# Causal linear attention in quadrants of the TensorE array, with the quotients taken on GpSimd

## The chip, the cores and the metric

The kernel runs on one core of a Trainium2 chip. The metric is the device time of one execution in microseconds (us). The engines are TensorE (PE; its weight loads are PEld), VectorE (DVE), ScalarE (ACT), GpSimd (POOL) and SyncE (SP), each with its own in-order instruction stream; they wait for each other on semaphores.

## The reference

One decoder block over x of 128 sequences x 64 tokens x 128 features, 16 heads of 8 features: causal linear attention, a second attention over a context, and a layer of 8 experts with 2 taken per token. Only the first part is touched:

```
q, k = f(xn @ wq + bq), f(xn @ wk + bk)       f(x) = x + 1 where x > 0, else exp(x)
v    = xn @ wv + bv                           xn = layernorm(x)
S_t = sum over s <= t of k_s (x) v_s          z_t = sum over s <= t of k_s     (per head)
out_t = (q_t . S_t) / (q_t . z_t + 1e-6);     x = x + out @ wo + bo
```

## The kernel before

Tokens lie in 64 tiles of 128 (two sequences of 64 tokens each); four tiles (GT = 4) are a group, 16 groups in all. The work is a pipeline by slots, written out by hand for every engine (`slot(n, i)`): in slot n the engines do projections and features of group n+1 ("a1"), statistics and normalization of group n+2 ("a0"), running sums of group n ("b"), quotients and output projection of group n-1 ("c"), and the keys and gram matrices of the second attention for group n-2 ("d"). `slots` unrolls the first and last slots and loops over the middle. Each engine goes through its list strictly in order, so an instruction that waits holds everything behind it.

For tile t = 4g + k:

- TensorE `project` (L1344) makes q, k, v of the tile in one PSUM bank (384 columns). ScalarE `a_evac_proj` (L642) takes them out with two relus, a copy of v and an exp (L647 to L653).
- GpSimd `features` (L528) adds both halves to f(q), f(k) (`qk`, L534); `outer_product` (L536) multiplies the key with v and with a ninth column of ones (`v9`, L542), which gives 16 x 9 x 8 = 1152 products per token.
- TensorE `running_sums` (L1336) multiplies them by the lower triangle `tri_s` (block diagonal: two sequences), in three matmuls of 432, 360 and 360 columns into three PSUM banks (`HEADS`).
- VectorE `times_q` (L887) multiplies them by q, in three pieces (L896), and `sum_heads` (L900) sums over 8 (L905) into `nd`: 8 numerators and one denominator per head.
- A slot later, ScalarE `denominators` (L655) adds the epsilon, VectorE `inverses` (L927) takes the reciprocal, and VectorE `quotients` (L932) multiplies (L935); TensorE transposes the quotients (`transposes`, L1331), ScalarE copies them out (`oT`, L693), TensorE projects them and VectorE adds them to X (`add_attention`, L939).

What sets the order near the change: on TensorE a slot is: transposes of the next group's xh, running sums of tile 1, project 0, the second attention's keys (L1384), project 1, transposes of the quotients, running sums of tile 2, output projection, project 2, transposes of xh2, running sums of tile 3, project 3, running sums of tile 0 of the next group, gram. On ScalarE: xT, denominators, evacuation of project 0, oT (waits for the transposed quotients), evacuation 1, normalization of xh2 (L668, L671), k2T, x2T, evacuation 2, normalization of xh, evacuation 3, gd. On GpSimd: features 0, `variance` (L515, waits for the moments of L877), outer 0, features 1, `root` (L522), outer 1, features 2, variance, outer 2, features 3, root, outer 3.

`settle` (L296) raises a semaphore that nothing waits for. `need` waits only where the count is positive.

## Time and profile before

| | us |
|---|---|
| median of 3 runs (lowest, highest) | 632.59 (632.16, 632.62) |
| span of the profiled execution, first to last instruction | 631.7 |
| the attention stage in it | from about 18 to 270 |

The profiled execution has no time of its own beside its span; the three runs were timed without a profile, and the median is 0.9 us above the span, which is what lies around it. "Busy" is the union of an engine's instructions. A row of the timeline gives the start in us from the start of the span, the length in us, the engine, line, operation, out<-in, the count merged, and in brackets how long the engine had been idle before and what ended that. A matmul on fp32 data is recorded as two passes, each with its own weight load; rows of matmuls hold the time in which the last result drains.

### The profile page before, as it was taken

How to read it: one execution, taken by the hardware profiler on the slowest of the kernel's cores; microseconds unless marked ns; L12 is line 12 of the kernel's file. 1: busy time of each engine (PE TensorE's matmuls, PEld its weight loads, DVE VectorE, ACT ScalarE, POOL GpSimd, SP SyncE). 2: the span in 40 equal slices, each digit the busy share in tenths (PEclk: the TensorE clock that was granted, in tenths of full speed). 3: DMA queues.
4: the chain of work that ended last, by engine and by line, in shares of the span. 5: the costliest groups of instructions: out<-in, count | busy, mean ns of one | idle time of the engine just before them, and what ended most of it. 6: DMA issues, size and time to landing. Idle time of an engine off the chain costs nothing.

```text
span 631.7 us, 15833 instructions
## 1 busy us (share of the span) xinstructions
PE 575.6 (91%) x3838; PEld 442.8 (70%) x3839; DVE 517.9 (82%) x1602; ACT 420.2 (67%) x1188; POOL 427.0 (68%) x461
## 2 busy tenths in 40 slices
PE   3899999999999999968799877999999999999993
PEld 1455555555555555545689644799999999989993
DVE  5599999999999999983678888566877887877883
ACT  3557777877787777351788512345788888878882
POOL 2899989998999899310877600765467666757762
PEclk9999999999999999999999968899999999999998
DMA  5610111111161111283477551221012111111110
GB/s 147 184 51 0 35 33 35 34 33 33 33 100 33 34 33 34 66 119 90 119 208 202 113 113 29 53 51 46 27 49 54 48 47 47 51 38 51 51 44 23
DMA packets 49973, 40.92 MB, mean 65 GB/s; under 512 B 21971, under 2 KB 40278, under 8 KB 49926
## 3 DMA queue, kind: packets, MB, share of 16 engines
q1 hardware_dynamic: 44150, 29.61, 19.0%
q0 software_dynamic: 4960, 10.49, 6.4%
q8 instruction: 20, 0.33, 0.2%
q10 hardware_dynamic: 816, 0.26, 0.2%
q14 instruction: 27, 0.22, 0.1%
HBM read 27.47 MB, written 12.88 MB: 64 GB/s over the span
## 4 chain that ended last, share of the span: by engine, by line
PE 63%; ACT 12%; DVE 12%; issue 6%; DMA 4%; POOL 1%; DVEq 0%; ACTq 0%; SPq 0%; POOLq 0%
PE bank L1329 57%; PE bank L1333 4%; ACT xh L671 3%; ACT xs L773 2%; PE bank L1568 2%; DMA w_s<-gram_d 1%; DVE on L935 1%; ACT ex L647 1%; ACT nb_c L668 1%; DVE mean_early L1037 1%; DMA circ<-prob_d 1%; PE bank L1492 1%; ACT rl L648 1%; ACT xrT L759 1%; ACT ex L653 1%
## 5 line engine op out<-in xcount | busy, mean ns | idle before, releaser
L542 POOL TENSOR_TENSOR shared<-v,qk 128x1152 f32<-128x1152 f32 x64 | 142.8, 2231 | 2.8
L1329 PE MATMUL bank<-shared,tri_s 128*128 128x360 f32 (+1 forms) x384 | 137.2, 494 | 0.7 <-DVE R L896 0.7
L609 POOL DMA_INDIRECT shared<-xs_d,row_u x91 | 87.8, 964 | 62.2 <-DVE row_u L1227 31.6
L896 DVE TENSOR_TENSOR R<-bank,qk 128x360 f32<-128x360 f32 (+1 forms) x192 | 96.2, 540 | 8.6 <-PE bank L1329 6.7
L1329 PEld LDWEIGHTS bank<-shared,tri_s 128*128 128x128 f32 x384 | 69.8, 192 | 44.9 <-issue 20.4
L616 POOL DMA_INDIRECT out_x<-shared x64 | 63.6, 993 | 48.4 <-DVE shared L1299 21.8
L905 DVE TENSOR_REDUCE nd<-R 128x144 f32<-128x1152 f32 x64 | 86.1, 1346 | 1.6
L1329 PE MATMUL bank<-w_s,hid 128*128 (+1 forms) x620 | 82.3, 276 | 0.1
L1329 PEld LDWEIGHTS bank<-w_s,hid 128*128 128x128 f32 x620 | 75.5, 192 | 0.6 <-issue 0.3
L812 ACT ACTIVATE shared<-bank 128x256 f32<-128x256 f32 x155 | 59.4, 384 | 21.9 <-PE bank L1329 16.2
L1320 DVE TENSOR_TENSOR hid<-bank,shared 128x256 f32<-128x256 f32 x155 | 61.4, 422 | 10.0 <-ACT shared L812 9.8
L1329 PE MATMUL bank<-shared,ct 128*128 128x128 f32 x512 | 67.8, 275 | 0.0
L1329 PE MATMUL bank<-shared,u 128*128 128x128 f32 x512 | 67.6, 275 | 0.0
L1329 PE MATMUL bank<-wqkv,xT 128*128 128x384 f32 x128 | 56.7, 526 | 6.9 <-ACT v L650 4.6
L1329 PEld LDWEIGHTS bank<-shared,ct 128*128 128x128 f32 x512 | 62.2, 192 | 0.3 <-issue 0.2
L1329 PEld LDWEIGHTS bank<-shared,u 128*128 128x128 f32 x512 | 62.3, 192 | 0.0
L802 ACT ACTIVATE shared<-bank,scale_s 128x128 f32<-128x128 f32 (+1 forms) x78 | 30.1, 386 | 41.1 <-PE bank L1568 41.1
L534 POOL TENSOR_TENSOR qk<-ex,rl 128x256 f32<-128x256 f32 x64 | 48.0, 751 | 9.7 <-ACT ex L653 9.6
L647 ACT ACTIVATE ex<-bank 128x256 f32<-128x256 f32 x64 | 24.1, 376 | 36.2 <-PE bank L1329 36.2
L1329 PEld LDWEIGHTS bank<-wqkv,xT 128*128 128x128 f32 x128 | 22.5, 198 | 29.7 <-ACT v L650 21.6
L806 ACT ACTIVATE ct<-w_s 128x512 f32 x64 | 39.7, 620 | 0.1
L1329 PE MATMUL bank<-ones 128*128 128x512 bf16 x128 | 36.0, 423 | 0.0
(247 smaller groups left out, 1138.4 us busy)
## 6 DMA issues: line engine op xcount, KB each, us to landing
xs_d<-xs SPq DMA_DIRECT2D x16, 270.0 KB, 4.7
X<-in_x SPq DMA_DIRECT2D x16, 256.0 KB, 2.8
ct<-in_ctx_t SPq DMA_DIRECT2D x16, 256.0 KB, 2.8
ct<-in_ctx_r SPq DMA_DIRECT2D x16, 256.0 KB, 3.6
gram_d<-gd SPq DMA_DIRECT2D x14, 256.0 KB, 2.4
w_s<-in_w_experts SPq DMA_DIRECT2D x8, 384.0 KB, 4.0
circ<-prob_d SPq DMA_DIRECT2D x30, 64.0 KB, 2.7
shared<-xs_d,row_u POOLq DMA_INDIRECT x91, 2.6
```

The lines of the kernel that those rows point to most:

```text
L534: nc.gpsimd.tensor_tensor(qk[p][:, k, :], ex[k % 2][:], rl[k % 2][:], ALU.add).then_inc(a_f, 1)
L542: nc.gpsimd.tensor_tensor(outer[k], v9[k % 2][:].unsqueeze(3).broadcast_to([P, H, D1, D]), kk.unsqueeze(2).broadcast_to([P, H, D1, D]), AL ...
L609: nc.gpsimd.indirect_dma_start(xg[q], None, xs_d[:, :], bass.IndirectOffsetOnAxis(ap=rows, axis=0)).then_inc(xg_in[q], 16)
L616: nc.gpsimd.indirect_dma_start(out[:, :], bass.IndirectOffsetOnAxis(ap=xg[(NXI + j) % NX][:, DEST:DEST + 1].bitcast(U32), axis=0), yg[q], ...
L647: nc.scalar.activation(ex[k % 2][:], bank[1][:, 0:2 * E], ACT.Relu, scale=-1.0).then_inc(a_pev, 1)
L802: nc.scalar.activation(xgT[p][:, cols], bank[0][:, cols], ACT.Copy, scale=scale_s[:, 0:1]).then_inc(x_xT, 1)
L806: nc.scalar.activation(w_tile[n % 2][0], w_s[:, dyn(held[0] * W_E, 2 * HID)], ACT.Copy).then_inc(x_wa, 1)
L812: nc.scalar.activation(silu[p][h], bank[1 + 2 * p + h][:, HID:2 * HID], ACT.Silu).then_inc(x_silu, 2 // len(items_of(i, up[0])))
L896: nc.vector.tensor_tensor(R[:, lo:hi], bank[2 + c][:, 0:n_h * D1 * D].rearrange("p (h e d) -> p h e d", h=n_h, e=D1), qq.unsqueeze(2).broa ...
L905: nc.vector.tensor_reduce(nd[p][:, k], R[:], AX.X, ALU.add).then_inc(b_red, 1)
L1320: nc.vector.tensor_tensor(hid[p][h][:], bank[1 + 2 * p + h][:, 0:HID], silu[p][h], ALU.mult).then_inc(x_h, 2 // len(items_of(i, j)))
L1329: return nc.tensor.matmul(o, l, r, start=start, stop=stop, skip_group_check=True)
```

## The change

The ninth column goes: `v8` holds v alone, an outer product has 1024 products per token, and the two running-sum banks `run` take the place of three. `running_sums` becomes four matmuls of 512 columns, each on 64 rows and 64 columns of the array: for sequence b of the tile and half c of the heads, from partitions of b to partitions of c. So partitions hold (half of the heads, token) and columns hold (sequence, ...). q is projected in the same layout by four matmuls of 64 columns, k and v as before by one of 256. `times_q` is one instruction per tile, `sum_heads` sums 1024 to 128. The denominators come apart from this: `key_sums` runs once per group on TensorE, at the slot's head ahead of the running sums of tile 1, waits for the features of all four tiles and sums the keys (four matmuls of 256 columns into bank 4); VectorE `key_dots` multiplies them by q and `sum_dots` sums them; ScalarE adds the epsilon in the group's own slot, behind evacuation 2, and VectorE takes the inverses in front of the last `sum_heads`. `quotients` is the first instruction of GpSimd's slot. `turn_quotients` turns them back with 16 matmuls of 64 columns by the identity in place of four transposes.

```diff
@@ -127,16 +126,16 @@
         xh = sb("xh", [P, GT, E])
         xT = sb("xT", [P, GW])
         ex, rl = [sb(f"ex{i}", [P, 2 * E]) for i in range(2)], [sb(f"rl{i}", [P, 2 * E]) for i in range(2)]
-        v9 = [sb(f"v9_{i}", [P, H, D1]) for i in range(2)]
+        v8 = [sb(f"v8_{i}", [P, E]) for i in range(2)]
         qk = [sb(f"qk{i}", [P, GT, 2 * E]) for i in range(2)]
 
-        shared = sb("shared", [P, GT * H * D1 * D])
+        shared = sb("shared", [P, 9 * GT * E])
         bias_f, bias_r, bias_a, bias_b = (shared[0:3, i * NBIAS:(i + 1) * NBIAS] for i in range(4))
         b_wide = shared[:, 4 * NBIAS:4 * NBIAS + 3 * E]
-        outer = [shared[:, i * H * D1 * D:(i + 1) * H * D1 * D].rearrange("p (h e d) -> p h e d", h=H, e=D1)
-                 for i in range(GT)]
-        R = sb("R", [P, H, D1, D])
-        nd = [sb(f"nd{i}", [P, GT, H, D1]) for i in range(2)]
+        outer = [shared[:, i * D * E:(i + 1) * D * E] for i in range(GT)]
+        R = sb("R", [P, (D + 1) * E])
+        num = [sb(f"num{i}", [P, GT, E]) for i in range(2)]
+        zq = sb("zq", [P, GT * E])
         den, rden = sb("den", [P, GT * H]), sb("rden", [P, GT * H])
         on = sb("on", [P, GT, E])
         oT = sb("oT", [P, GW])
...
@@ -537,11 +541,20 @@
                 t = GT * g + k
                 pool.wait_ge(a_f, t + 1)
                 pool.wait_ge(a_pev, 3 * t + 3)
-                need(pool, b_run, 3 * (t - GT) + 3)
+                need(pool, b_run, t - GT + 1)
                 kk = qk[p][:, k, E:2 * E].rearrange("p (h d) -> p h d", h=H)
+                vv = v8[k % 2][:].rearrange("p (h e) -> p h e", h=H)
                 nc.gpsimd.tensor_tensor(
-                    outer[k], v9[k % 2][:].unsqueeze(3).broadcast_to([P, H, D1, D]),
-                    kk.unsqueeze(2).broadcast_to([P, H, D1, D]), ALU.mult).then_inc(a_outer, 1)
+                    outer[k].rearrange("p (h e d) -> p h e d", h=H, e=D), vv.unsqueeze(3).broadcast_to([P, H, D, D]),
+                    kk.unsqueeze(2).broadcast_to([P, H, D, D]), ALU.mult).then_inc(a_outer, 1)
+
+            def quotients(g, p, r):
+                pool.wait_ge(c_rden, g + 1)
+                need(pool, c_tr, g)
+                pool.wait_ge(b_red, GT * g + GT)
+                nc.gpsimd.tensor_tensor(
+                    on[:].rearrange("p t (h d) -> p (t h) d", h=H), num[p][:].rearrange("p t (h d) -> p (t h) d", h=H),
+                    rden[:].unsqueeze(2).broadcast_to([P, GT * H, D]), ALU.mult).then_inc(c_on, 1)
 
             def slot(n, i):
                 a0, a1, c = stage(n, i, 2), stage(n, i, 1), stage(n, i, -1)
...
@@ -549,6 +562,8 @@
                 of_c = c and (c[0], c[1], mv_c, c_mv, ve_c, c_ve, rs_c, c_rs, d_xh)
                 if i is None and n == -1:
                     pool.wait_ge(bias_ch, 8)
+                if c:
+                    quotients(*c)
                 if a1:
                     features(*a1, 0)
                 if a0:
...
@@ -647,15 +662,13 @@
                 nc.scalar.activation(ex[k % 2][:], bank[1][:, 0:2 * E], ACT.Relu, scale=-1.0).then_inc(a_pev, 1)
                 nc.scalar.activation(rl[k % 2][:], bank[1][:, 0:2 * E], ACT.Relu).then_inc(a_pev, 1)
                 need(act, a_outer, t - 1)
-                nc.scalar.activation(v9[k % 2][:, :, 0:D], bank[1][:, 2 * E:3 * E].rearrange("p (h d) -> p h d", h=H),
-                                     ACT.Copy).then_inc(a_pev, 1)
+                nc.scalar.activation(v8[k % 2][:], bank[1][:, 2 * E:3 * E], ACT.Copy).then_inc(a_pev, 1)
                 act.wait_ge(a_pev, 3 * t + 1)
                 nc.scalar.activation(ex[k % 2][:], ex[k % 2][:], ACT.Exp, scale=-1.0).then_inc(a_ex, 1)
 
             def denominators(g, p, r):
-                act.wait_ge(b_red, GT * g + GT)
-                need(act, c_rden, g)
-                nc.scalar.activation(den[:], nd[p][:, :, :, D].rearrange("p t h -> p (t h)"), ACT.Copy, bias=ATT_EPS).then_inc(c_den, 1)
+                act.wait_ge(b_dots, 2 * g + 2)
+                nc.scalar.activation(den[:], den[:], ACT.Copy, bias=ATT_EPS).then_inc(c_den, 1)
 
             def negative_mean(g, p, mv, mv_sem, mr, mr_sem):
                 act.wait_ge(mv_sem, GT * g + GT)
...
@@ -681,8 +694,6 @@
                     nc.scalar.activation(wvo_s[:], bank[1][:, 0:E], ACT.Copy).then_inc(fold_w, 1)
                 if a1:
                     a_evac_xT(*a1)
-                if c:
-                    denominators(*c)
                 if d:
                     negative_mean(d[0], d[1], mv_c, c_mv, mr_c, c_mr)
                 if a1:
@@ -705,6 +716,8 @@
                     nc.scalar.activation(x2T[:], bank[5][:], ACT.Copy).then_inc(d_xT, 1)
                 if a1:
                     a_evac_proj(*a1, 2)
+                if b:
+                    denominators(*b)
                 if a0:
                     g, p, r = a0
                     need(act, a_tr, g)
...
@@ -884,25 +897,35 @@
                 for k in range(GT):
                     nc.vector.bn_aggr(mv_e[:, GT * g + k, :], st_e[:, k, :]).then_inc(e_mv, 1)
 
-            def times_q(g, p, r, k, pieces):
+            def times_q(g, p, r, k):
                 t = GT * g + k
-                if pieces[0] == 0:
-                    need(dve, b_red, t)
-                for c in pieces:
-                    lo, hi = HEADS[c]
-                    n_h = hi - lo
-                    dve.wait_ge(b_run, 3 * t + c + 1)
-                    qq = qk[p][:, k, lo * D:hi * D].rearrange("p (h d) -> p h d", h=n_h)
-                    nc.vector.tensor_tensor(
-                        R[:, lo:hi], bank[2 + c][:, 0:n_h * D1 * D].rearrange("p (h e d) -> p h e d", h=n_h, e=D1),
-                        qq.unsqueeze(2).broadcast_to([P, n_h, D1, D]), ALU.mult).then_inc(b_mul, 1)
+                need(dve, b_red, t)
+                dve.wait_ge(b_run, t + 1)
+                qq = qk[p][:, k, 0:E].rearrange("p (h d) -> p h d", h=H)
+                nc.vector.tensor_tensor(
+                    R[:, 0:D * E].rearrange("p (h e d) -> p h e d", h=H, e=D),
+                    run[:].rearrange("p (h e d) -> p h e d", h=H, e=D),
+                    qq.unsqueeze(2).broadcast_to([P, H, D, D]), ALU.mult).then_inc(b_mul, 1)
 
             def sum_heads(g, p, r, k):
                 t = GT * g + k
-                dve.wait_ge(b_mul, 3 * t + 3)
+                dve.wait_ge(b_mul, t + 1)
                 if k == 0:
                     need(dve, c_on, g - 1)
-                nc.vector.tensor_reduce(nd[p][:, k], R[:], AX.X, ALU.add).then_inc(b_red, 1)
+                nc.vector.tensor_reduce(num[p][:, k, :], R[:, 0:D * E].rearrange("p (x d) -> p x d", d=D), AX.X, ALU.add
+                                        ).then_inc(b_red, 1)
+
+            def key_dots(g, p, r):
+
+                dve.wait_ge(b_keys, g + 1)
+                nc.vector.tensor_tensor(
+                    zq[:].rearrange("p (k b x) -> p b k x", k=GT, b=2), bank[4][:].rearrange("p (b k x) -> p b k x", b=2, k=GT),
+                    qk[p][:, :, 0:E].rearrange("p k (b x) -> p b k x", b=2), ALU.mult).then_inc(b_dots, 1)
+
+            def sum_dots(g, p, r):
+                dve.wait_ge(b_dots, 2 * g + 1)
+                need(dve, c_rden, g)
+                nc.vector.tensor_reduce(den[:], zq[:].rearrange("p (x d) -> p x d", d=D), AX.X, ALU.add).then_inc(b_dots, 1)
 
             def split_fold():
 
...
@@ -946,23 +962,18 @@
             def slot(n, i):
                 a0, a1, b, c = (stage(n, i, s) for s in (2, 1, 0, -1))
                 if b:
-                    times_q(*b, 0, (0, 1, 2))
+                    times_q(*b, 0)
                 if b:
                     sum_heads(*b, 0)
-                if c:
-                    inverses(*c)
-                if b:
-                    times_q(*b, 1, (0,))
-                if c:
-                    quotients(*c)
-                if b:
-                    times_q(*b, 1, (1, 2))
+                    key_dots(*b)
+                    times_q(*b, 1)
                 if a0:
                     g, p, r = a0
                     dve.wait_ge(x_in[p], 16 * r + 16)
                     stats(g, p, st_a, a_st, mv_a, a_mv, a_nb, GT)
                 if b:
                     sum_heads(*b, 1)
+                    sum_dots(*b)
                 if a0:
                     moments(a0[0], a0[1], st_a, a_st, mv_a, a_mv, a_nb, GT)
                 if i is None and n == FIRST:
...
@@ -984,11 +995,11 @@
                     dve.wait_ge(c_x1, c[0] + 1)
                     stats(c[0], c[1], st_c, c_st, mv_c, c_mv, c_nb, GT)
                 if b:
-                    times_q(*b, 3, (0,))
+                    times_q(*b, 3)
                 if c:
                     moments(c[0], c[1], st_c, c_st, mv_c, c_mv, c_nb, GT)
                 if b:
-                    times_q(*b, 3, (1, 2))
+                    inverses(*b)
                     sum_heads(*b, 3)
 
...
@@ -1333,20 +1344,49 @@
                     last = nc.tensor.transpose(o[:, k * P:(k + 1) * P], src[:, k, :], id_s[:])
                 return last
 
+            def turn_quotients():
+
+                settle(pe)
+                for k in range(GT):
+                    for b in range(2):
+                        for c in range(2):
+                            own = slice(c * HALF, c * HALF + HALF)
+                            last = mm(bank[5][own, k * P + b * HALF:k * P + b * HALF + HALF],
+                                      on[own, k, b * HALF:b * HALF + HALF], id_s[own, own])
+                return last
+
             def running_sums(g, p, r, k):
                 t = GT * g + k
                 pe.wait_ge(a_outer, t + 1)
-                for c, (lo, hi) in enumerate(HEADS):
-                    need(pe, b_mul, 3 * (t - 1) + c + 1)
-                    mm(bank[2 + c][:, 0:(hi - lo) * D1 * D], tri_s[:], outer[k][:, lo:hi].rearrange("p h e d -> p (h e d)")
-                       ).then_inc(b_run, 1)
+                need(pe, b_mul, t)
+                settle(pe)
+                for b in range(2):
+                    for c in range(2):
+                        own = slice(b * L, b * L + L)
+                        last = mm(run[c * L:c * L + L, b * 512:b * 512 + 512], tri_s[own, own], outer[k][own, c * 512:c * 512 + 512])
+                last.then_inc(b_run, 1)
+
+            def key_sums(g, p, r):
+
+                pe.wait_ge(a_f, GT * g + GT)
+                need(pe, b_dots, 2 * g - 1)
+                for b in range(2):
+                    for c in range(2):
+                        last = mm(bank[4][c * L:c * L + L, b * GT * HALF:(b + 1) * GT * HALF], tri_s[:, b * L:b * L + L],
+                                  qk[p][:, :, E + c * HALF:E + c * HALF + HALF])
+                last.then_inc(b_keys, 1)
 
             def project(g, p, r, k):
                 t = GT * g + k
                 if k == 0:
                     pe.wait_ge(a_xT, g + 1)
                 need(pe, a_pev, 3 * t)
-                mm(bank[1][:, 0:3 * E], xT[:, k * P:(k + 1) * P], wqkv[:]).then_inc(a_proj, 1)
+                mm(bank[1][:, E:3 * E], xT[:, k * P:(k + 1) * P], wqkv[:, E:3 * E])
+                for b in range(2):
+                    for c in range(2):
+                        last = mm(bank[1][c * L:c * L + L, b * HALF:b * HALF + HALF], xT[:, k * P + b * L:k * P + b * L + L],
+                                  wqkv[:, c * HALF:c * HALF + HALF])
+                last.then_inc(a_proj, 1)
 
             def keep_warm(of, times):
 
...
@@ -1370,6 +1410,7 @@
                     need(pe, a_xT, a1[0])
                     transposes(bank[0], xh).then_inc(a_tr, 1)
                 if b:
+                    key_sums(*b)
                     running_sums(*b, 1)
                 if a1:
                     if i is None and a1[0] == 0:
...
@@ -1385,11 +1426,11 @@
                 if a1:
                     project(*a1, 1)
                 if i is None and n == NG:
-                    pe.wait_ge(b_mul, 3 * NT)
+                    pe.wait_ge(b_mul, NT)
                     keep_warm(2, 10)
                 if c:
                     pe.wait_ge(c_on, c[0] + 1)
-                    transposes(bank[5], on).then_inc(c_tr, 1)
+                    turn_quotients().then_inc(c_tr, 1)
                 if i is None and n == NG:
                     keep_warm(2, 2)
                 if b:
```

## Rows read from the trace of the kernel before

**Rows 1.** The page of the profile: busy time of the engines over the span.
```profile
PE 575.6 (91%) x3838; PEld 442.8 (70%) x3839; DVE 517.9 (82%) x1602; ACT 420.2 (67%) x1188; POOL 427.0 (68%) x461
...
PE 63%; ACT 12%; DVE 12%; issue 6%; DMA 4%; POOL 1%; DVEq 0%; ACTq 0%; SPq 0%; POOLq 0%
```

**Rows 2.** Engines by stretch: busy of PE, PEld, DVE, ACT, POOL; clock; DMA share; GB/s.
```profile
60.00:100.00 40.00, 38.44 (x188) 22.63 (x188) 38.97 (x89) 32.23 (x106) 35.88 (x31) 1.00 0.09 27
```

**Rows 3.** Timeline, feature tile 3 of groups 1, 2, 14, 15 on POOL: start, us.
```profile
39.51 0.73 POOL L534 TENSOR_TENSOR qk<-ex,rl 128x256 f32<-128x256 f32 x1
...
53.81 0.72 POOL L534 TENSOR_TENSOR qk<-ex,rl 128x256 f32<-128x256 f32 x1
...
239.93 0.73 POOL L534 TENSOR_TENSOR qk<-ex,rl 128x256 f32<-128x256 f32 x1
...
253.30 0.73 POOL L534 TENSOR_TENSOR qk<-ex,rl 128x256 f32<-128x256 f32 x1
```

**Rows 4.** Timeline of one slot, TensorE from one gram to the quotients, and ScalarE.
```profile
66.22 0.69 PE L1329 MATMUL bank<-x2T,k2T 128*64 128x64 f32 x16
...
66.83 0.66 PE L1333 MATMUL bank<-id_s,xh 128*128 128x128 f32 x4
...
67.33 2.10 PE L1329 MATMUL bank<-shared,tri_s 128*128 128x432 f32 x6
...
68.02 0.31 ACT L658 ACTIVATE den<-nd 128x64 f32<-128x64 f32 x1
...
69.26 0.81 PE L1329 MATMUL bank<-wqkv,xT 128*128 128x384 f32 x2
...
69.91 1.02 PE L1329 MATMUL bank<-ct,wkk 128*128 128x512 f32 x2
70.11 0.38 ACT L647 ACTIVATE ex<-bank 128x256 f32<-128x256 f32 x1 [1.68 <-PE bank L1329]
...
70.99 0.91 PE L1329 MATMUL bank<-wqkv,xT 128*128 128x384 f32 x2
...
71.74 0.60 PE L1333 MATMUL bank<-id_s,on 128*128 128x128 f32 x4
...
72.38 0.60 ACT L693 ACTIVATE oT<-bank 128x512 f32<-128x512 f32 x1 [1.14 <-PE bank L1333]
```

**Rows 5.** The same timeline, later: the rest of the slot on ScalarE, VectorE, GpSimd.
```profile
71.22 0.86 DVE L869 BATCH_NORM_STATS2 st_a<-X 128x6 f32<-128x128 f32 x4
...
72.00 1.33 DVE L905 TENSOR_REDUCE nd<-R 128x144 f32<-128x1152 f32 x1
...
73.25 0.37 DVE L877 BATCH_NORM_AGGREGATE mv_a<-st_a 128x2 f32<-128x6 f32 x4
...
73.81 0.19 POOL L520 TENSOR_SCALAR ve_a<-mv_a 128x4 f32<-128x4 f32 x1 [0.66 <-ACT v L650]
...
81.33 1.49 DVE L896 TENSOR_TENSOR R<-bank,qk 128x432 f32<-128x432 f32 x3
...
81.78 0.41 ACT L653 ACTIVATE ex<-ex 128x256 f32<-128x256 f32 x1
...
82.02 0.66 PE L1333 MATMUL bank<-id_s,xh 128*128 128x128 f32 x4
...
83.26 0.73 POOL L534 TENSOR_TENSOR qk<-ex,rl 128x256 f32<-128x256 f32 x1
```

**Rows 6.** Groups of instructions, 60 to 246 us: count, busy us, mean ns, idle before.
```profile
L935 DVE TENSOR_TENSOR on<-nd,rden 128x512 f32<-128x512 f32 x12 | 13.8, 1150 | 0.0
...
L526 POOL TENSOR_TENSOR rs_a<-ve_a,power 128x4 f32<-128x4 f32 x12 | 12.2, 1021 | 0.0
```

**Rows 7.** Timeline: the quotients on VectorE beside an outer product on GpSimd.
```profile
84.94 2.17 POOL L542 TENSOR_TENSOR shared<-v,qk 128x1152 f32<-128x1152 f32 x1
...
85.12 2.53 DVE L935 TENSOR_TENSOR on<-nd,rden 128x512 f32<-128x512 f32 x1
```

**Rows 8.** Timeline of the last slots: the last quotients and what follows them.
```profile
269.68 0.60 ACT L693 ACTIVATE oT<-bank 128x512 f32<-128x512 f32 x1 [1.96 <-PE bank L1333]
```

More of the change, by code:

```diff
@@ L53 @@
 PITCH = L * (2 * L + 1)
-HEADS = [(0, 6), (6, 11), (11, 16)]
+HALF = E // 2
 def need(eng, sem, count):
@@ L221, in build @@
         is_row = [halves(shared[:, SORT + i * NSORT * NT:SORT + (i + 1) * NSORT * NT], PAIRS, 2, NT, 2) for i in range(2)]
-        is_tile = [halves(R[:].rearrange("p h e d -> p (h e d)")[:, i * PAIRS * NT:(i + 1) * PAIRS * NT], PAIRS, NT, 2)
+        is_tile = [halves(R[:][:, i * PAIRS * NT:(i + 1) * PAIRS * NT], PAIRS, NT, 2)
                    for i in range(2)]
-        row_t = R[:].rearrange("p h e d -> p (h e d)")[:, NSORT * NT:NSORT * NT + P]
+        row_t = R[:][:, NSORT * NT:NSORT * NT + P]
         xg = [shared[:, i * ROW:(i + 1) * ROW] for i in range(NX)]
@@ L236, in build, with psum @@
         y0 = sb("y0", [P, E])
-        bank = [ctx.enter_context(nc.psum_tensor(f"bank{i}", [P, 512], F32)) for i in range(8)]
+        def psum(name, banks=1):
+            return ctx.enter_context(nc.psum_tensor(name, [P, banks * 512], F32))
+        bank = [psum("bank0"), psum("bank1")]
+        run = psum("run", 2)
+        bank += [run[:, i * 512:(i + 1) * 512] for i in range(2)] + [psum(f"bank{i}") for i in range(4, 8)]
         settled = sem("settled")
@@ L256, in build @@
         b_run, b_mul, b_red = sem("b_run"), sem("b_mul"), sem("b_red")
+        b_keys, b_dots = sem("b_keys"), sem("b_dots")
         c_den, c_rden, c_on, c_tr, c_oT, c_y, c_x1, c_st, c_mv, c_ve, c_rs = (
@@ L505, in _ @@
             pool.memset(power[:], -0.5).then_inc(setup, 1)
-            for k in range(2):
-                pool.memset(v9[k][:], 1.0).then_inc(setup, 1)
             pool.memset(ones_f[:], 1.0).then_inc(setup, 1)
@@ L512, in _ @@
             pool.memset(used[0][:], 0.0).then_inc(s_used, 1)
-            pool.wait_ge(setup, 5)
+            pool.wait_ge(setup, 3)
             def variance(g, p, stats, seen, ve, ve_sem, rs, rs_sem, normed):
@@ L531, in features @@
                 pool.wait_ge(a_ex, t + 1)
-                need(pool, b_mul, 3 * (t - 2 * GT) + 3)
+                need(pool, b_mul, t - 2 * GT + 1)
+                need(pool, b_dots, 2 * (g - 1) - 1)
                 need(pool, a_outer, t - 2 * GT + 1)
@@ L674, in slot @@
             def slot(n, i):
-                a0, a1, c, d = (stage(n, i, s) for s in (2, 1, -1, -2))
+                a0, a1, b, c, d = (stage(n, i, s) for s in (2, 1, 0, -1, -2))
                 if i is None and n == 1:
@@ L930, in inverses @@
                 nc.vector.reciprocal(rden[:], den[:]).then_inc(c_rden, 1)
-            def quotients(g, p, r):
-                dve.wait_ge(c_rden, g + 1)
-                need(dve, c_tr, g)
-                nc.vector.tensor_tensor(
-                    on[:].rearrange("p t (h d) -> p (t h) d", h=H), nd[p][:, :, :, 0:D].rearrange("p t h d -> p (t h) d"),
-                    rden[:].unsqueeze(2).broadcast_to([P, GT * H, D]), ALU.mult).then_inc(c_on, 1)
             def add_attention(g, p, r):
@@ L977, in slot @@
                 if b:
-                    times_q(*b, 2, (0, 1, 2))
+                    times_q(*b, 2)
                 if c:
@@ L1006, in _ @@
             nc.vector.tensor_scalar(rev[:], iota_s[:, 0:NE], -1.0, float(NE), ALU.mult, ALU.add).then_inc(setup, 1)
-            dve.wait_ge(setup, 12)
+            dve.wait_ge(setup, 10)
             dve.wait_ge(s_used, 1)
@@ L1439, in _ @@
             pe.wait_ge(const_in, 64)
-            pe.wait_ge(setup, 5)
+            pe.wait_ge(setup, 3)
             mm(bank[1][:, 0:3 * E], ones_f[:], wqkv[:]).then_inc(w_mean, 1)
@@ L1450, in v_product @@
                 last.then_inc(e_v, 1)
-            pe.wait_ge(b_mul, 3 * NT)
+            pe.wait_ge(b_mul, NT)
             pe.wait_ge(fold_w, 1)
@@ L1515, in cross_slot @@
                         keep_warm(0, 3)
-            pe.wait_ge(setup, 11)
+            pe.wait_ge(setup, 9)
             cross_slots(cross_slot)
```

1 line of the change is left out of this document (removed).

## The prediction

> **What bounds the kernel now.** I read the page first. TensorE has the largest busy share and the largest share of the chain [rows 1], but that mixes stages; the change touches the attention stage alone, so the table of engines by stretch counts. There TensorE is busy 38.4 us of 40, VectorE 39.0, GpSimd 35.9, ScalarE 32.2, at the full granted clock [rows 2]. Two engines are full, so taking work from both looks like a sure gain. The length of a slot comes from a fixed mark: the fourth features instruction of a group on GpSimd (F3 below) starts at 53.81 for group 2 and at 239.93 for group 14 [rows 3]: 186.1 us for 12 slots, **15.51 us a slot**. The timeline of one slot then shows who waits for whom. ScalarE goes from oT (72.38) to the last exp of project 3 (81.78 + 0.41 = 82.19) in 9.81 us, nearly all of it its own work [rows 4, 5]. VectorE reaches its next slot at 81.33; F3 ends only at 83.26 + 0.73 = 83.99, though its input was there at 82.19, because GpSimd was in an outer product; and TensorE starts its slot with transposes at 82.02 [rows 5]. So a group's last features come 2.0 us *after* TensorE has entered the slot of that group. Today this costs nothing: the running sums of tile 1 need only tile 1.
>
> **By busy time** the change gains. An outer product takes 2.17 us for 1152 elements [rows 7] and a features instruction 0.73 for 256 [rows 3]: 1.61 ns an element beside 0.32 fixed. So 1024 elements cost 1.97 us, and the quotients (512) 1.14; bounds are 0.96 (share of an outer product) and 1.46 (twice features), and I take the line through both. GpSimd has per slot 4 x 1.97 + 4 x 0.73 + 2 roots of 1.02 [rows 6] + 2 x 0.19 [rows 5] + 1.14 = 14.4 us. VectorE: busy 15.1 (0.974 x 15.51); three pieces of times_q take 1.49 together [rows 5], so one of 1024 costs 1.49 less 0.13 less two starts of 0.1 = 1.17: minus 1.3 per slot; four sums of 128 x 8 instead of 144 x 8 save 0.13 each: 0.5; the quotients go, 1.15 on average [rows 6], since some of them last 2.53 beside an outer product [rows 7]; two new instructions of 512 add about 0.68 each. Sum 13.5. TensorE: a full-array pass of 512 columns takes (1.02 - 0.17)/2 = 0.43, where 0.17 is the drain by which neighbours overlap (67.33 + 2.10 against 69.26) [rows 4]. The gram's 16 passes of 64 columns would take 16 x 0.053 = 0.86 in a row, but take 0.69 - 0.17 = 0.52 [rows 4]: its two column halves run at once. For the row halves no row exists. Bounds for the four quadrants' running sum: 0.87 (all four at once, two passes of 0.43) and 1.73 (only column pairs); I take 0.87, as the gram's pairs overlap almost fully. After the gram, neighbours overlap by 0.08, not 0.17 (66.22 + 0.69 against 66.83) [rows 4]: I take 0.1 for each change of the array's shape. There are some 14 more per slot. TensorE comes to about 13 us. So no engine is fuller than 14.4 of today's 15.5.
>
> **By the round trip** it loses, and that decides. `key_sums` stands at the head of TensorE's slot and waits for F3; behind it in the same queue are running sums 1, project 0, project 1 and the turning of the quotients, for which ScalarE's oT waits; and behind oT are 9.81 us of ScalarE work that end in the exp that the *next* F3 needs. Everything is in order, so this is a closed circle of one slot. From the end of F3, in us: 0.10 to wake TensorE and load; keys 0.86 (four matmuls of 256 columns, two at once, two passes of 0.213); 0.10 shape; running sum 0.87; 0.10; k and v 0.43; 0.10; q 0.23; 0.21 drain and wake; ScalarE's relus and v copy with the wake 0.88 (70.11 to 70.99) [rows 4]; project 1 0.43 + 0.10 + 0.23; 0.10; turning 0.93 (16 matmuls, two passes of 0.053 to 0.058, two quadrants at once, where four transposes took 0.44); 0.21. Sum **5.88** to the start of oT. Before, without keys and shapes, transposes to oT took 66.83 to 72.38. Then 9.81, plus 0.31 for the epsilon instruction, now inside that stretch [rows 4], 0.05 to wake, 0.73 for F3: 5.88 + 9.81 + 0.31 + 0.05 + 0.73 = **16.78 us a slot**.
>
> The other engines fit in. Quotients: GpSimd after F3 has a root 1.02, outer 1.97, quotients 1.14: ready at 4.2, before TensorE gets there (4.8). So moving them neither gains nor loses in a full slot; cover 0.6 us. GpSimd with VectorE makes a second circle: F3, keys, running sum, times_q 1 at 2.14; then 1.17, statistics 0.78, sum 1.12, denominators' sum 0.68, moments 0.56 to the variance [rows 5]; from variance to F3's end 10.18 (73.81 to 83.99) less three shortenings of 0.2: 9.57. Sum 16.0, also above 15.51. It sets a slot where ScalarE has less: slot 1 (before: 53.81 - 39.51 = 14.30) and slot 14 (253.30 - 239.93 = 13.37) [rows 3], which I put at 16.0 and 15.9.
>
> Sum: 12 x (16.78 - 15.51) = +15.2; slot 1 +1.7; slot 14 +2.5; two shorter outer products ahead of the first F3, -0.4. The end, from F3 of group 15 (254.03) to the last oT (269.68) [rows 3, 8]: shorter by three tiles of 0.45 and the denominators' 0.8, longer by keys 0.96, turning 0.5, quotients 0.46 and a wake: no difference. Setup loses two small fills of `v9`, covered by loads. After 270 us nothing changes. +19.0 on the profiled 631.7 and so on the median of 632.6 (0.9 above it): **651.6 us**.
>
> **Rivals.** (a) Quadrants that share one bank are not written at once: turning takes 1.8, 0.9 more on the circle, 13 slots and the end: +13, 664 us. For it: both turning quadrants write bank 5 from different rows of the array; against: the gram's halves share bank 6 and overlap [rows 4], though from the same rows. The page TensorEngine Tiling (Array Packing) of the Trainium skill, Restrictions and Gotchas, says that different row tiles cannot access one PSUM bank simultaneously; no row of before shows it. (b) Row halves don't overlap anywhere: also +0.87 for running sum 1, and TensorE itself fills: 18.6 us a slot, about 676. (c) **Faster**, one mechanism: the wait of the keys doesn't bind, because F3 is there when TensorE has done its transposes. Then GpSimd's 14.4 sets the slot: 12 x (14.4 - 15.5) and 2 at the ends, about 617. It decides once F3 ends before about 0.5 after TensorE's slot begins; today it ends 2.0 after, 1.1 of which is GpSimd's lateness, and the 0.73 and the exp before it can't go. (d) The circle is 1.3 shorter than I add up (no cost of shapes, shorter wakes, gains of the ends): no change.
>
> **Numbers.** The forecast case 0.62, (a) 0.14, (b) 0.09, (c) 0.10, (d) 0.05. Small terms: without shape costs the circle is 16.2 (-8 us, and -2 at slots 1 and 14): 641; (a) with slower quotients (1.46) 668. Range 641 to 668; it leaves out (b), (c), (d) in the main. 0.2% is what a measurement of this kernel can tell from no change. Slower 0.86, same 0.03, faster 0.11.
>
> **What would show it.** In the profile after: F3 to F3 at 16.8; "PE <- POOL qk" as a large new wait in front of the keys' weight load, some 1 us a slot; VectorE busy near 80% in the stretch, idle in front of key_dots; ScalarE's wait for oT longer; running sum of a tile about 1.04 long in place of 2.10; quotients on GpSimd 1.14 and ahead of TensorE. I am wrong if keys are found without a wait, if F3 follows GpSimd's own work rather than the exp, or if slots are below 15.5.

## The result, and the profile after

The median after is 663.35 us (662.79 to 666.04, four runs) against 632.54 before: ratio 1.0489 [1.0466, 1.0512]. The forecast was slower, 651.6 us, range 641 to 668: the sign and the range hold, but the loss is 30.8 us, not 19.0. The profiled span grew from 631.7 to 661.4, by 29.7.

The page after, for [rows 1], with the groups of the changed work (busy us, mean ns | idle before, releaser):

```profile
PE 563.1 (85%) x5054; PEld 418.3 (63%) x5055; DVE 498.8 (75%) x1490; ACT 417.3 (63%) x1188; POOL 425.6 (64%) x475
...
PE 39%; DVE 8%; ACT 3%; DMA 3%; issue 2%; POOL 1%; DVEq 0%; ACTq 0%; SPq 0%; POOLq 0%
...
L547 POOL TENSOR_TENSOR shared<-v,qk 128x1024 f32<-128x1024 f32 x64 | 125.0, 1953 | 2.8
L905 DVE TENSOR_TENSOR R<-run,qk 128x1024 f32<-128x1024 f32 x64 | 78.4, 1224 | 45.4 <-PE run L1340 43.8
...
L915 DVE TENSOR_REDUCE num<-R 128x128 f32<-128x1024 f32 x64 | 76.8, 1200 | 1.1
```

Engines by stretch after (length; busy of PE, PEld, DVE, ACT, POOL; clock, DMA share, GB/s), for [rows 2]:

```profile
60.00:100.00 40.00, 34.22 (x365) 18.19 (x365) 32.62 (x68) 26.55 (x91) 31.98 (x31) 1.00 0.09 28
...
180.00:220.00 40.00, 33.59 (x318) 16.45 (x316) 31.04 (x63) 24.86 (x84) 30.85 (x28) 0.96 0.33 63
```

No engine is full any more: VectorE fell from 39.0 to 32.6 of 40 us, and the kernel is slower. Who waits, 60 to 260 us (total us, times, longest):

```profile
ACT ex L662 <- PE bank L1340: 41.8, 12, 4.9
DVE R L905 <- PE run L1340: 28.1, 35, 1.5
ACT oT L704 <- PE bank L1340: 23.9, 12, 2.0
...
PE bank L1340 <- POOL qk L538: 14.9, 11, 1.4
```

The last row is the wait of the keys: 11 slots of some 1.3 us. The first and third are where ScalarE pays for it: 3.5 us a slot in front of project 0's relu and 2.0 in front of oT, where the same view of the kernel before has 20.6 and 16.4 us in all, 1.7 and 1.4 a slot. One turn of the circle, from the timeline, from F3 to the next F3:

```profile
91.05 0.72 POOL L538 TENSOR_TENSOR qk<-ex,rl 128x256 f32<-128x256 f32 x1 [0.37 <-ACT ex L667]
...
91.91 1.08 PE L1340 MATMUL bank<-qk,tri_s 128*64 128x256 f32 x8 [1.22 <-POOL qk L538]
...
92.92 1.09 PE L1340 MATMUL run<-shared,tri_s 64*64 64x512 f32 x8
...
93.94 1.08 PE L1340 MATMUL bank<-wqkv,xT 128*128 128x256 f32 x10
94.64 1.07 POOL L555 TENSOR_TENSOR on<-num,rden 128x512 f32<-128x512 f32 x1
...
95.15 0.38 ACT L662 ACTIVATE ex<-bank 128x256 f32<-128x256 f32 x1 [3.11 <-PE bank L1340]
...
96.03 1.08 PE L1340 MATMUL bank<-wqkv,xT 128*128 128x256 f32 x10
...
97.04 1.08 PE L1340 MATMUL bank<-id_s,on 64*64 64x64 f32 x29
...
98.31 0.60 ACT L704 ACTIVATE oT<-bank 128x512 f32<-128x512 f32 x1 [2.04 <-PE bank L1340]
...
107.86 0.41 ACT L667 ACTIVATE ex<-ex 128x256 f32<-128x256 f32 x1
...
108.51 0.73 POOL L538 TENSOR_TENSOR qk<-ex,rl 128x256 f32<-128x256 f32 x1 [0.61 <-DVE R L905]
```

Read downwards, this is the forecast's chain link by link: F3 ends at 91.77, the keys start at 91.91, and everything up to oT follows without a gap of its own; ScalarE needs 9.96 us from oT to the end of the exp, and F3 comes 0.24 later. The quotients are ready at 95.71, ahead of TensorE's 97.04. F3 starts at 39.35 for group 1, 56.94 for group 2, 266.81 for group 14 and 283.46 for group 15: slot 1 is 17.59 us, slot 14 is 16.65, and the 12 between are **17.49** on average (209.87 in all) (forecast 16.0, 15.9 and 16.78; before [rows 3] 14.30, 13.37 and 15.51).

### The profile page after: what moved, and what is told of

It reads as the page before. It is cut to its first block, busy times and chain, and to the rows that moved or that the text cites. A ratio compares the mean times of both kernels' runs of the same rounds, so it can differ in the third digit from the quotient of the medians.

```text
span 661.4 us, 18060 instructions
## 1 busy us (share of the span) xinstructions
PE 563.1 (85%) x5054; PEld 418.3 (63%) x5055; DVE 498.8 (75%) x1490; ACT 417.3 (63%) x1188; POOL 425.6 (64%) x475
## 4 chain that ended last, share of the span: by engine, by line
PE 39%; DVE 8%; ACT 3%; DMA 3%; issue 2%; POOL 1%; DVEq 0%; ACTq 0%; SPq 0%; POOLq 0%
PE bank L1340 25%; PE run L1340 11%; ACT xs L786 2%; PE bank L1609 2%; DMA w_s<-gram_d 1%; DVE mean_early L1048 1%; PE run L1533 1%; DVE st_e L895 1%; ACT xrT L772 1%; DVE X L1169 1%; DMA circ<-prob_d 0%; DMA shared<-xs_d,row_u 0%; DMA gram_d<-gd 0%; POOL rs_e L605 0%; DVE base L1209 0%
## 5 line engine op out<-in xcount | busy, mean ns | idle before, releaser
L547 POOL TENSOR_TENSOR shared<-v,qk 128x1024 f32<-128x1024 f32 x64 | 125.0, 1953 | 2.8
L905 DVE TENSOR_TENSOR R<-run,qk 128x1024 f32<-128x1024 f32 x64 | 78.4, 1224 | 45.4 <-PE run L1340 43.8
L1340 PEld LDWEIGHTS bank<-wqkv,xT 128*64 128x64 f32 (+1 forms) x640 | 41.0, 153 | 72.2 <-issue 37.5
L1340 PE MATMUL bank<-wqkv,xT 128*64 128x64 f32 (+1 forms) x640 | 71.3, 280 | 10.8 <-ACT v L665 10.0
L915 DVE TENSOR_REDUCE num<-R 128x128 f32<-128x1024 f32 x64 | 76.8, 1200 | 1.1
L1340 PE MATMUL run<-shared,tri_s 64*64 64x512 f32 x512 | 72.9, 632 | 1.6 <-issue 1.5
L1331 DVE TENSOR_TENSOR hid<-run,shared 128x256 f32<-128x256 f32 x78 | 33.0, 423 | 7.8 <-ACT shared L825 7.4
L825 ACT ACTIVATE shared<-run 128x256 f32<-128x256 f32 x78 | 29.8, 382 | 10.9 <-PE run L1340 7.7
L825 ACT ACTIVATE shared<-bank 128x256 f32<-128x256 f32 x77 | 29.5, 383 | 10.6 <-PE bank L1340 8.4
L1340 PE MATMUL run<-shared,ct 128*128 128x128 f32 x256 | 33.9, 275 | 0.1
L1340 PE MATMUL run<-shared,u 128*128 128x128 f32 x256 | 33.8, 275 | 0.0
```

The costliest lines, as they stand in the source:

```text
L547: nc.gpsimd.tensor_tensor(outer[k].rearrange("p (h e d) -> p h e d", h=H, e=D), vv.unsqueeze(3).broadcast_to([P, H, D, D]), kk.unsqueeze(2 ...
L825: nc.scalar.activation(silu[p][h], bank[1 + 2 * p + h][:, HID:2 * HID], ACT.Silu).then_inc(x_silu, 2 // len(items_of(i, up[0])))
L905: nc.vector.tensor_tensor(R[:, 0:D * E].rearrange("p (h e d) -> p h e d", h=H, e=D), run[:].rearrange("p (h e d) -> p h e d", h=H, e=D), q ...
L915: nc.vector.tensor_reduce(num[p][:, k, :], R[:, 0:D * E].rearrange("p (x d) -> p x d", d=D), AX.X, ALU.add).then_inc(b_red, 1)
L1331: nc.vector.tensor_tensor(hid[p][h][:], bank[1 + 2 * p + h][:, 0:HID], silu[p][h], ALU.mult).then_inc(x_h, 2 // len(items_of(i, j)))
L1340: return nc.tensor.matmul(o, l, r, start=start, stop=stop, skip_group_check=True)
```

## The experiments

Theory C (the closed circle of the forecast) says that a slot is F3, keys, TensorE's order up to oT, and ScalarE's order up to the next F3. The rivals were that GpSimd's new piece costs the time, and that the narrow matmuls do. All kernels start from the changed one unless said otherwise; ratios are to the kernel before on the same chip. In the cuts of code, words in round brackets and behind `#` stand for lines or places that are not printed.

**The keys later.** On TensorE behind the running sums of tile 2; their multiply and sum on VectorE behind those of tile 2.

```diff
-                    key_sums(*b)
                     running_sums(*b, 1)
...
                     running_sums(*b, 2)
+                    key_sums(*b)
```

> Edit to the changed kernel: the key sums go behind the running sums of tile 2 on TensorE, key_dots and sum_dots behind times_q 2 and sum_heads 2 on VectorE. Theory (circle through the keys' wait): features no longer hold TensorE's slot head. The circle of 17.4 us opens; the next one goes oT, 9.9 us of ScalarE, features 3, root, outer product, quotients on GpSimd (0.2 + 0.7 + 1.0 + 1.95 + 1.1), turning 1.3: about 16.3 us a slot, 13 slots: 648 us (644 to 653). Rival (the many small matmuls and their changes of shape fill TensorE): the place of the keys doesn't matter, 660 or more. Rival (VectorE and GpSimd set the slot): no change either.

Measured 645.87 us (643.87 to 646.47), ratio 1.0202 [1.0180, 1.0224]. oT comes every 16.13 to 16.28 us in place of 17.4. The place of one wait costs 17.5 us of the 30.8. The matmuls of the keys are all still there, so this is the wait and not their work; what remains is +13. Some 1.6 of the 17.5 comes from the clock: this trace has one stretch at a lower clock, the changed kernel has two (both told further below).

**The quotients back on VectorE,** behind the first `times_q`; the keys stay at the head.

```diff
-                if c:
-                    quotients(*c)        # GpSimd, slot's head
...
                     times_q(*b, 0)
+                if c:
+                    quotients(*c)        # VectorE
```

> Edit to the changed kernel: the quotients alone go back to VectorE, behind times_q 0; the rest stays. Theory (circle through the keys): quotients are ready before TensorE gets to them on either engine, so 663 us within 4. Rival (quotients at GpSimd's slot head cost the time): back to about 640.

Measured 672.98 us (669.55 to 674.10), ratio 1.0619 [1.0587, 1.0651]: 9.6 *above* the changed kernel, where no difference was expected. The timeline shows F3 and the quotients side by side:

```profile
93.23 1.28 POOL L538 TENSOR_TENSOR qk<-ex,rl 128x256 f32<-128x256 f32 x1 [0.37 <-ACT ex L657]
93.25 0.68 DVE L949 TENSOR_TENSOR on<-num,rden 128x512 f32<-128x512 f32 x1
...
94.64 1.08 PE L1340 MATMUL bank<-qk,tri_s 128*64 128x256 f32 x8 [1.78 <-POOL qk L538]
```

Here F3 takes 1.28 us in place of 0.73, on the circle. This is the worst slot: where the quotients start some 0.25 before F3, as in nine of the slots, F3 takes 1.02 to 1.03:

```profile
111.00 0.68 DVE L949 TENSOR_TENSOR on<-num,rden 128x512 f32<-128x512 f32 x1
...
111.25 1.02 POOL L538 TENSOR_TENSOR qk<-ex,rl 128x256 f32<-128x256 f32 x1 [0.60 <-DVE R L895]
```

Ordinary slots are 17.68 to 17.85 us, 0.3 longer like F3: some 3.7 us in 12 slots. Five of the slots are 18.98 to 19.35; in each of them the granted clock falls. The trace has four such stretches more than that of the changed kernel, at some 1.6 us each: 6.4 of the 10.9 us by which the two profiled spans differ. In the changed kernel the move of the quotients is thus worth 9.6 us, which the forecast put at nothing, but only some 3.7 us of it are the collision of the two engines.

**Both together.**

> Edit to the changed kernel: keys late and quotients on VectorE, both. Theory: both circles through GpSimd are open; the rest is oT, ScalarE up to the normalized group (8.9), transposes, running sum 1, project 0, ScalarE, project 1, turning: about 15.7 us a slot, 640 us (634 to 646), below keys late alone by some 8. Rival (VectorE and GpSimd set the slot, where the quotients on VectorE collide with outer products): not below keys late alone.

Measured 639.48 us (638.79 to 640.61), ratio 1.0111 [1.0094, 1.0128]. With late keys the quotients on VectorE are 6.4 us *better* than on GpSimd (645.87), with early keys 9.6 worse: what the move is worth hangs on which circle binds. Here the slots alternate between 15.99 and 16.19, not the 15.7 expected: with F3 off the path, the one pair of `run` banks binds, since a running sum waits until VectorE has multiplied the one before:

```profile
116.12 1.23 DVE L895 TENSOR_TENSOR R<-run,qk 128x1024 f32<-128x1024 f32 x1
...
117.49 1.09 PE L1340 MATMUL run<-shared,tri_s 64*64 64x512 f32 x8 [0.89 <-DVE R L895]
```

**The quotients alone, on the kernel before,** at the head of GpSimd's slot.

> Edit to the kernel before: only the quotients go to GpSimd's slot head. Theory: the circle oT, 9.8 us of ScalarE, features 3 to quotients on GpSimd (5.2), turning (0.75) is about 15.7 to 15.9 a slot against 15.5: 635 to 640 us. Rival (VectorE was the bound and is freed of 1.15 us a slot, collisions included): 620 to 628.

Measured 637.78 us (636.95 to 639.76), ratio 1.0090 [1.0067, 1.0112]. The busiest engine is relieved and the kernel loses 5 us. GpSimd is busy 37.9 of 40 us in the stretch of [rows 2], in place of 35.9, and slots go to 15.75.

**q in the old layout:** one projection of 384 columns. `times_q` then multiplies by q of other tokens and heads, so the attention's values differ; every instruction keeps its shape.

```diff
-                mm(bank[1][:, E:3 * E], xT[:, k * P:(k + 1) * P], wqkv[:, E:3 * E])
-                (four matmuls of 64 columns)
+                mm(bank[1][:, 0:3 * E], xT[:, k * P:(k + 1) * P], wqkv[:]).then_inc(a_proj, 1)
```

> Edit to the changed kernel: q, k and v of a tile again by one matmul of 384 columns (q then lies in the old layout, so the attention is not the reference's; no instruction but the projection changes). Two projections lie on the circle; from their start to ScalarE's first relu they now take 1.21 us against 0.85 before, and from project 1 to the turning 1.01 against 0.75. Theory (the circle's terms add): 0.62 us a slot less, 16.8 us a slot, 13 slots: 663.4 - 8 = 655 (652 to 658). Rival (TensorE's total work sets the slot): all four projections count, 1.45 us a slot less, 644.

Measured 659.40 us (657.72 to 660.69), ratio 1.0410 [1.0376, 1.0445], above both expectations and 1.4 outside the range of the first.

```profile
94.46 0.91 PE L1340 MATMUL bank<-wqkv,xT 128*128 128x384 f32 x2
...
96.37 0.91 PE L1340 MATMUL bank<-wqkv,xT 128*128 128x384 f32 x2
97.21 1.08 PE L1340 MATMUL bank<-id_s,on 64*64 64x64 f32 x29
```

From project 1 to the turning it is 0.84 us where it was 1.01, from project 0 to the relu 1.03 (in the same timeline the relu starts at 95.49) where it was 1.21: q's own matmuls cost 0.17 to 0.18 a tile against one wide one, and the slot falls by 0.37 (17.42 to 17.05), where 0.62 was expected: that took both stretches back to their lengths before, 0.85 and 0.75. In the kernel before the same wide project 1 takes 0.75 to the transposes behind it, without a change of shape [rows 4: 70.99 to 71.74]. So 0.09 of the 0.84 is the change of shape, as the forecast's 0.10 has it.

**Running sums on the full array:** two matmuls of 512 columns in place of four, which leaves the sums in the old layout of partitions.

> Edit to the changed kernel: the running sums by two matmuls of 512 columns on the whole array in place of four in the quadrants (the sums then lie in the old layout, so the attention is not the reference's). One running sum lies on the circle: 4 x 0.43 = 1.71 us of streaming in place of about 0.92, a change of shape less. Theory: 0.7 us a slot more, 672 us (668 to 677). Rival (the quadrants don't run at once, or their gain lies elsewhere): no change, 661 to 665. Rival (TensorE full): four running sums count, 2.8 us a slot, 700.

Measured 674.62 us (674.08 to 675.84), ratio 1.0666 [1.0635, 1.0697]; slots 18.14, +0.72. So the four quadrants run at once, and the one running sum on the circle is 0.7 shorter by them. Of the change's parts this is the one that pays where it binds.

**Late keys, and the quotients on GpSimd behind F3 of the slot before** in place of the head.

> Edit to the kernel with late keys: GpSimd takes the quotients of the finished group behind features 3, ahead of the root and the last outer product, no longer at the next slot's head. Theory (second circle, through root and outer product ahead of the quotients): it opens as it did with quotients on VectorE, 639 us or a little less, since VectorE loses 0.8 us a slot of work (636 to 641). Rival (GpSimd's total work sets the slot): as with late keys alone, 646.

Measured 640.19 us (639.37 to 642.74), ratio 1.0129 [1.0093, 1.0165]: 5.7 less than with the quotients at the head. At the head they stood between an outer product and the next slot's first features with no gap on either side (in the run with late keys 105.76 to 106.79), and so made GpSimd late by their own length.

**A new order.** On top of that: the second attention's keys and project 0 ahead of the running sum of tile 1, ScalarE's copy of the gram behind the first evacuation of the next slot, features wait for the exp last; two more slots are written out ahead of the loop.

```diff
-                    running_sums(*b, 1)
-                    project(*a1, 0)
                     (keys of the second attention)
+                    project(*a1, 0)
+                    running_sums(*b, 1)
                     project(*a1, 1)
```

> Edit to the kernel of the run before this one: on TensorE the second attention's keys and project 0 go ahead of running sum 1, which had waited for times_q 0; ScalarE's gram copy goes behind evacuation 0 of the next slot, into its wait; features wait for the exp last; the loop over slots starts two slots later. Theory (what is left is ScalarE's own chain: oT to the last exp 9.9, xT 0.6, project 0 1.2, evacuation 0.9, project 1 1.0, turning 1.3 = 14.9, and VectorE's 14.2 with its waits): 15.2 us a slot, 626 to 633. Rival (the chain stays on VectorE and running sums, one buffer for both): 636 to 640.

Measured 627.05 us (624.78 to 629.50), ratio 0.9897 [0.9865, 0.9929]. Slots are 14.72 us where written out and 15.0 to 15.2 in the loop. With this order the changed kernel beats the one before by 1.0%.

**The same order on the kernel before,** as a control.

> Edit to the kernel before (full-array sums, quotients on VectorE): the same new order as in the reordered kernel, as a control: the second attention's keys and project 0 ahead of running sum 1, the gram copy behind evacuation 0, the loop two slots later. Theory: before is held by TensorE's 14.9 us and VectorE's 15.1 us of work in a slot of 15.5, so an order that shortens ScalarE's round trip gives little: 628 to 634. Rival (the order alone makes the gain of the reordered kernel): 627 or less.

Measured 635.43 us (631.89 to 637.46, ten runs), ratio 1.0034 [1.0015, 1.0053], just above the range expected. Its ordinary slots are 15.0 to 15.2 and two are 16.9. So the order alone gains nothing in the whole; it needs the room that the change made. In its trace groups 2 to 14 take 184.2 us in place of 186.1, a gain of 1.9 us, and slot 1 takes 16.4 in place of 14.3 at a granted clock of 0.58 (40 to 44 us), a loss of the same size. The control lacks the late wait of the features, which by itself shows no gain (last run).

**The new order without a loop:** all slots written out.

```diff
-            for n in range(FIRST, 6):
-                slot(n, None)
-            with eng.Fori(3, (NG - 2) // 2) as i:
-                slot(0, i)
-                slot(1, i)
-            for n in range(NG - 2, LAST + 1):
+            for n in range(FIRST, LAST + 1):
```

> Edit to the reordered kernel: no loop over slots, all are written out. In its trace the written-out slots take 14.72 us, those in the loop 15.08 (waits against registers stand on the circle). Theory: 8 slots of 0.36 us: 3 us less, 624 (621 to 626). Rival (the longer program costs its own fetches): 627 or more.

Measured 622.96 us (621.44 to 626.17), ratio 0.9837 [0.9801, 0.9874], the fastest of all. oT comes every 14.72 to 14.73 us, slot after slot. Three engines are at 37 to 38 of 40 us, against 32 to 34 in the changed kernel:

```profile
100.00:140.00 40.00, 37.79 (x410) 20.28 (x409) 36.78 (x77) 32.04 (x108) 37.65 (x36) 1.00 0.14 41
```

**The features' wait for the exp last,** alone on the changed kernel.

```diff
-                pool.wait_ge(a_ex, t + 1)
                 (the other waits)
+                pool.wait_ge(a_ex, t + 1)
                 nc.gpsimd.tensor_tensor(qk[p][:, k, :], ex[k % 2][:], rl[k % 2][:], ALU.add)
```

> Edit to the changed kernel: in features the wait for the exp stands last, behind the three waits that are long fulfilled. In the changed kernel's trace features 3 starts 0.24 to 0.37 us behind the exp's end. Theory (that start lies on the circle): 0.2 us a slot less, 660.5 (659 to 662). Rival: no change, 663.4.

Measured 663.98 us (661.18 to 665.02), ratio 1.0471 [1.0444, 1.0498]: no gain to be seen. The slots are 17.22 and 17.39 in turn in place of 17.38 and 17.46, about 0.1 shorter, but two of them are 18.8 and 19.0, where the changed kernel had one of 19.05. A gain of 1 us is less than the 1.6 that one such slot costs. Inconclusive.

## Why the prediction was right, and why 12 us short

**The chain was right, its links were too short.** The circle by links, in us: the forecast, a written-out slot (F3 at 74.00 and 91.05) and a loop slot (the one shown above).

| link | forecast | written out | loop |
|---|---|---|---|
| F3 end to keys | 0.10 | 0.05 | 0.14 |
| keys to running sum 1 | 0.96 | 1.02 | 1.01 |
| running sum 1 to project 0 | 0.97 | 1.01 | 1.02 |
| project 0 to relu | 0.97 | 1.13 | 1.21 |
| relu to project 1 | 0.88 | 0.88 | 0.88 |
| project 1 to turning | 0.86 | 1.01 | 1.01 |
| turning to oT | 1.14 | 1.20 | 1.27 |
| oT to end of exp | 10.12 | 9.95 | 9.96 |
| exp to F3 | 0.05 | 0.07 | 0.24 |
| F3 | 0.73 | 0.73 | 0.72 |
| slot | 16.78 | 17.05 | 17.46 |

The rows of the written-out slot that the shown ones don't cover:

```profile
74.00 0.73 POOL L538 TENSOR_TENSOR qk<-ex,rl 128x256 f32<-128x256 f32 x1 [0.37 <-ACT ex L667]
...
74.78 1.08 PE L1340 MATMUL bank<-qk,tri_s 128*64 128x256 f32 x8 [1.15 <-POOL qk L538]
...
77.94 0.38 ACT L662 ACTIVATE ex<-bank 128x256 f32<-128x256 f32 x1 [2.97 <-PE bank L1340]
...
79.83 1.08 PE L1340 MATMUL bank<-id_s,on 64*64 64x64 f32 x29
...
81.03 0.60 ACT L704 ACTIVATE oT<-bank 128x512 f32<-128x512 f32 x1 [1.96 <-PE bank L1340]
```

Three terms failed, one by its size and two that were put at nothing:

1. *The length of a projection.* The forecast summed 0.76 for either projection, 0.12 above the 0.64 that the wide project 0 takes [rows 4: 69.26 to 69.91]. q's own matmuls cost 0.17 (the run with q in the old layout), and project 1 takes 0.10 more than project 0 already in the kernel before [rows 4: 70.99 to 71.74]; why is not shown. That is the 0.15 of the row "project 1 to turning". For project 0 it is 0.16: 0.06 from q's matmuls and 0.10 because a wide projection behind a narrow running sum takes 0.91 with its drain (the run with q in the old layout), where it took 0.81. "I take 0.1 for each change of the array's shape", from one pair of neighbours, holds in front of the turning (0.09). The rest of TensorE's part is 0.16 too short in small bits, less 0.05 at the first wake; ScalarE's part was 0.17 too long, since the epsilon instruction costs 0.15 (in the written-out slot it starts at 87.13 and the next one at 87.28), not 0.31. Together +0.27.
2. *The loop.* The forecast took its durations from rows of a written-out slot [rows 4] and used them for all. In the loop each of the four wakes on the circle costs more: 0.09, 0.08, 0.07 and 0.17, together the 0.41 between the two columns. That loop slots cost more is also seen without this circle: with the new order the eight slots in the loop are together 2.5 us longer than the same eight written out; the other 1.6 of the 4.1 us gained by writing out lies outside them and was not taken apart. Why a wake takes longer there is not shown; there the wait compares with a count that runs in the loop.
3. *Two slots at a lower clock.* One slot lasts 19.04 us. In its stretch of 40 us the granted clock is 0.96; from 198 to 200 us it is 0.50, which is 1.2 GHz in place of 2.4, and a running sum there takes 1.99 us in place of 1.09. TensorE had waited 1.39 us for the keys just before, as it had in eight slots without a fall. The other is slot 1: the clock is 0.50 from 41 to 43 us (0.57 from 40 to 44), behind a wait of 2.24. What is lost there, 43% of 4 us or 1.7, is as much as that slot's whole miss (17.59 for 16.0); the kernel before is at 1.00 there. The stretch in slot 1 with its keys, then the rows of the slow slot:

```profile
40.00:44.00 4.00, 3.87 (x17) 1.30 (x18) 0.70 (x2) 0.00 (x0) 3.06 (x3) 0.57 0.00 0
...
40.13 1.97 PE L1340 MATMUL bank<-qk,tri_s 128*64 128x256 f32 x8 [2.24 <-POOL qk L538]
...
196.40 1.30 PE L1340 MATMUL bank<-qk,tri_s 128*64 128x256 f32 x8 [1.39 <-POOL qk L538]
...
197.63 1.99 PE L1340 MATMUL run<-shared,tri_s 64*64 64x512 f32 x8
```

The sum of the miss on the profiled span: two written-out slots of 12 at +0.27, nine loop slots at +0.63 and the slow one at +2.26 make 8.5; slot 1 (17.59 for 16.0) 1.6 and slot 14 (16.65 for 15.9) 0.7; the start gained 0.16, not 0.4, and the end gained 0.5, not nothing. That is 10.6 against 29.7 - 19.0 = 10.7. The median rose by 1.1 more than the span. So the lower clock made some 3.2 of it, the loop 3.6 and the links of point 1 3.2. Without its clock slot 1 is 15.9, the 16.0 of the second circle; slot 14 was not taken apart.

The lower end of the range took more off than its terms give: five changes of shape lie on the circle, so 16.3 and not 16.2, and 643 to 644 us in place of 641. Nothing hangs on it.

**The forecast's other steps.** *Costs on GpSimd and VectorE*: 1.97 for an outer product was 1.95, 1.14 for the quotients 1.07 (L555 above), 1.17 for `times_q` 1.22; the reduction takes 1.20. *Quadrants*: a running sum with its drain takes 1.09 (1.04 forecast; 2.10 before). *The place of the quotients*: "neither gains nor loses" holds for the slot as it is, where they are 1.3 us ahead of TensorE. But it compared with a VectorE on which they cost nothing to others; there they lengthen F3 by 0.3 in most slots and by 0.55 at most. [Rows 7] show that neighbourhood with GpSimd as the winner and VectorE as the loser (2.53); I did not ask what happens with the roles turned round. The Trainium skill, GPSIMD Engine Reference, Specifications, states the cause in general: the two share their SBUF interface when a VectorE instruction reads two SBUF inputs. The trace agrees: the quotients read `num` and `rden`, both in SBUF, and F3 beside them takes 1.02 to 1.28 for 0.73.

**The rivals.** (a) forecast 664 us, nearly what was measured, and is false all the same: by it the turning would take 1.8 us, and it takes 1.08 with its drain, though its quadrants write one bank from different rows of the array.

The Trainium skill, TensorEngine Tiling (Array Packing), Restrictions and Gotchas, says that different row tiles cannot access one PSUM bank at once; here the two also write different partitions of it, and they overlapped. A number that fits is no evidence for its mechanism; one row decided.

(b) falls by the running sum of 1.09 and by the full-array run. (c) fails in its condition: it needs F3's end within 0.5 us of the start of TensorE's transposes, and in the slot shown these start at 90.03 and F3 ends at 91.77, so the keys wait each time. Its price was of the right kind: where the keys don't wait and the quotients are out of the way, the slot is 14.72, near the 14.4 added up for GpSimd; which engine holds it there was not taken apart. (d) falls, the circle was longer.

**The base was mixed.** The 15.51 us before is no common slot either. Features of tile 1 start at 76.21 and 93.47 in the trace of before, a slot of 17.26, while most are 14.7 to 15.2; there are three like it. The median of the quotients before is 0.68 us, not the mean of 1.15 [rows 6] that the forecast took; the three at 2.53 to 2.59 [rows 7] stand in these three slots. With the quotients on GpSimd the kernel before has no such slot (15.5 to 16.0 from group 2 to 14), and as the control of the order it has two, again with the quotients at 2.55 and 2.72. Beside the others, about 14.95 long, the change costs some 2.5 us a slot.

**Where the 30.8 us are,** by the runs: the keys' wait at the slot's head 17.5; the quotients in front of the features 5.7 (with the keys late). The 7.6 left (640.19 against 632.54) was not taken apart; in the run with late keys and the quotients on VectorE (639.48) the one pair of `run` banks binds. The new order takes 13.1 back, more than that, and writing out the loop another 4.1.

## What to carry to other kernels

Before work is moved between engines, close the circle: follow a group from its last instruction through every queue that stands behind a new wait back to the same instruction, and compare that sum, not the busy shares, with the length of a slot. A relief shows only once the order lets it: the same edit was 4.9% slower at the slot's head and 1.0% faster with its wait moved back and the queues reordered, where the new order alone gave the kernel before nothing. (1.6% with the loop written out; the kernel before was not run without its loop.) Take durations for a loop from a slot in the loop, and price an instruction by what it does to its neighbour too, in both directions.

## What the runs showed of the hardware

- **The clock falls in single slots.** Now and then the granted clock falls to 0.50, in the changed kernel behind a wait of TensorE for the keys, and such a slot is 1.6 us longer (19.04 for 17.4). Between 36 and 284 us the changed kernel has two such stretches, the run with the quotients on VectorE, whose keys wait 1.5 to 2.6 us, has six, the run with late keys one; the kernel before and the new order without a loop have none. The same wait of 1.39 us stands in front of slots at full clock too, so what decides is not shown. What was added up from rows at full clock misses this.
- **The contention of GpSimd and VectorE goes both ways:** an `add` of 256 columns on GpSimd takes 1.02 to 1.28 for 0.73 us beside the quotients on VectorE, by how far the two overlap, and in the kernel before the quotients take 2.53 for 0.68 beside an outer product. Its three collisions of this kind fall into slots 2.3 us longer than their neighbours.
- **Four quadrants with fp32 data run at once:** the eight passes of a running sum last 1.09 us with the drain, two full-array matmuls in their place 1.88 to 1.98.
- **A wake costs 0.07 to 0.17 us more in the loop** than in a slot written out (one slot of each, link by link).
